# Reordering the start of a fused token-mixing and feed-forward kernel, and signalling its last step by tile

## The reference

```python
W = cond_weights[itok]                          # [32, 64, 64], picked out of [16, 64, 64]
y = einsum('bct,bcd->bdt', x, W)                # mixes the 64 rows of each sample
h = gelu(y @ inter_w + inter_b)                 # [1024] -> [4096], tanh approximation
out = x + h @ output_w + output_b               # [4096] -> [1024]
```

## Time and profile before

| | us |
|---|---|
| median of 3 runs (1271.19 to 1271.51) | 1271.4 |
| the profiled execution's own time | 1270.05 |
| its span in the profile | 1268.2 |
| TensorE busy in the span | 1251.0 |
| VectorE busy | 833.9 |
| ScalarE busy | 567.7 |
| GpSimd busy | 188.5 |

### The profile page before, as it was taken

One profiled execution on the slowest core, in us unless ns is written; L12 is line 12 of the kernel. 1 busy time (PEld: TensorE's weight loads), 2 busy tenths in 40 slices (PEclk: granted clock), 3 DMA queues, 4 the chain that ended last, 5 costly groups with the idle time before them and its releaser, 6 DMA issues.

```text
span 1268.2 us, 15308 instructions
## 1 busy us (share of the span) xinstructions
PE 1251.0 (99%) x5634; PEld 1039.4 (82%) x5634; DVE 833.9 (66%) x1086; ACT 567.7 (45%) x969; POOL 188.5 (15%) x94
## 2 busy tenths in 40 slices
PE   6999999999999999999999999999999999999998
PEld 6888888888888888888888888888888888888886
DVE  5888688676477777757656555555547767774764
ACT  3755445454444444444434444444444444444442
POOL 5242233212000000000033233222200000000000
PEclk9999999999999999999999999999999999999999
DMA  9396566763998232239835335553199942233531
GB/s 348 111 323 227 211 225 249 265 238 144 355 400 322 100 99 90 94 138 391 305 116 191 112 125 183 183 182 131 78 334 395 349 135 90 98 100 100 166 124 43
DMA packets 94941, 249.54 MB, mean 197 GB/s; under 512 B 8307, under 2 KB 16531, under 8 KB 93459
## 3 DMA queue, kind: packets, MB, share of 16 engines
q1 hardware_dynamic: 93778, 248.28, 54.1%
q10 hardware_dynamic: 1088, 0.28, 0.1%
HBM read 162.55 MB, written 85.98 MB: 196 GB/s over the span
## 4 chain that ended last, share of the span: by engine, by line
PE 95%; DVE 3%; DMA 1%; issue 1%; ACT 0%; SPq 0%; DVEq 0%; ACTq 0%
PE ps L558 48%; PE ps L542 45%; DVE lhs L774 1%; PE ps L502 1%; DVE y L763 1%; DMA y_mem<-y_out 1%; PE ps L487 1%; DMA x<-in_x_dram 0%; DVE hs L788 0%; DVE c L781 0%; ACT lhs L620 0%; DVE y_out L876 0%; ACT y_whole L589 0%; DVE acc L849 0%; ACT y L609 0%
## 5 line engine op out<-in xcount | busy, mean ns | idle before, releaser
L542 PE MATMUL ps<-y,lhs 128*128 128x512 f32 x2688 | 611.6, 389 | 2.8 <-ACT y_whole L589 1.5
L558 PE MATMUL ps<-rhs,lhs 128*128 128x512 f32 x2688 | 609.6, 389 | 0.0
L542 PEld LDWEIGHTS ps<-y,lhs 128*128 128x128 f32 x2688 | 503.9, 188 | 108.3 <-ACT y_whole L589 1.6
L558 PEld LDWEIGHTS ps<-rhs,lhs 128*128 128x128 f32 x2688 | 504.5, 188 | 104.8
L690 ACT ACTIVATE lhs<-h_raw 128x512 fp32r<-128x512 f32 x224 | 141.6, 632 | 345.8 <-PE ps L558 340.2
L833 DVE TENSOR_TENSOR lhs<-h_raw,lhs 128x512 fp32r<-128x512 f32 x224 | 155.0, 692 | 188.5 <-ACT lhs L690 188.5
L774 DVE TENSOR_TENSOR lhs<-w_raw,lhs 128x512 fp32r<-128x512 f32 x128 | 117.9, 922 | 127.7 <-ACT lhs L620 127.6
L620 ACT ACTIVATE lhs<-w_raw 128x512 fp32r<-128x512 f32 x128 | 80.8, 632 | 165.6 <-PE ps L542 161.8
L836 DVE TENSOR_TENSOR rhs<-W,rhs 128x512 fp32r<-128x512 f32 x224 | 153.3, 684 | 0.0
L774 DVE TENSOR_TENSOR lhs<-s_w,lhs 128x512 fp32r<-128x512 f32 x96 | 90.2, 940 | 88.2 <-ACT lhs L620 88.1
L458 POOL TENSOR_TENSOR s_w<-w_raw 128x1024 f32<-128x1024 f32 x16 | 48.1, 3008 | 636.7 <-PE ps L558 354.0
(11 more groups left out here) (34 smaller groups left out, 291.6 us busy)
## 6 DMA issues: line engine op xcount, KB each, us to landing
h_raw<-h_mem SPq DMA_DIRECT2D x112, 512.0 KB, 3.4
w_raw<-in_L_ffn_inter_w_dram SPq DMA_DIRECT2D x32, 1024.0 KB, 8.8
h_mem<-hs SPq DMA_DIRECT2D x64, 512.0 KB, 4.7
W<-in_L_ffn_output_w_dram SPq DMA_DIRECT2D x32, 1024.0 KB, 12.6
h_mem<-c SPq DMA_DIRECT2D x48, 512.0 KB, 5.8
y_mem<-y_out SPq DMA_DIRECT2D x28, 512.0 KB, 3.2
y<-y_mem SPq DMA_DIRECT2D x7, 2048.0 KB, 13.0
x<-in_x_dram SPq DMA_DIRECT2D x16, 512.0 KB, 12.3
```

What stands on the lines that cost most here:

```text
L542: last = nc.tensor.matmul(ps[:, bank, :], w[:, k, :], y[i][:, part, k, :], start=(i in FRESH and k == 0 and u == 0), stop=(k == KH - 1 and ...
L558: last = nc.tensor.matmul(ps[:, bank2(h, j, tb), :], lhs[s % RING][:, a, blk(tb)], rhs[r][:, w, :], start=(j in FRESH and q == 0 and u == ...
```

## The change

It has four parts.

1. The half of `cond_all` that SP issued goes to ACT, which now issues both. SP issues all eight tiles `x0` ahead of the first group's weights.
2. POOL waits, ahead of its four sums of the first group, until the first two chunks' weights have been split (`lhs_lo >= 2`).
3. The bias is turned behind the first chunk instead of ahead of all matmuls, with a wait until DVE has copied out all its banks of the mixing (it reuses bank 7). DVE's copy of it moves behind the first `y_sum`; `cond1(1)`, which writes that bank, waits for the copy.
4. In the last step of the kernel, TensorE signals after each of the four token blocks (`tile_done`), and each of DVE's last four additions waits for its own block. That step no longer counts in `step_done`.

```diff
--- before.py
+++ after.py
@@ -137,6 +137,7 @@
         cond_done = sem("cond_done")
         cond1_done = sem("cond1_done")
         step_done = sem("step_done")
+        tile_done = sem("tile_done")
 
         kept_act = sem("kept_act")
         y1_taken = sem("y1_taken")
@@ -305,11 +306,9 @@
                 sp.dma_start(y[i][:].bitcast(F32), y_mem[i]).then_inc(y_in[i], 16)
 
             sp.dma_start(itok_sb[0:1], itok.rearrange("(o b) -> o b", o=1)).then_inc(itok_in, 16)
-            sp.dma_start(cond_all[0:C], cond_w.rearrange("s c d -> c s d")).then_inc(cond_in, 16)
             for j in range(TILES):
                 sp.dma_start(x0[:, j, :], x_tok[0, :, j, :]).then_inc(x0_in[j], 16)
-                if j == TB - 1:
-                    load_w1(0, 0)
+            load_w1(0, 0)
             for j in range(TILES):
                 if j == TILES - 2:
                     sp.wait_ge(cond_done, 2 * KB)
@@ -455,6 +454,7 @@
                         pool.wait_ge(step_done, step2(h - 1, PRODUCTS, -2))
                     else:
                         pool.wait_ge(cond_done, KB)
+                        pool.wait_ge(lhs_lo, 2)
                     nc.gpsimd.tensor_tensor(s1_w[:], a21, a22, ALU.add).then_inc(s_made[0], 1)
                     if g > 0:
                         pool.wait_ge(lhs_lo, step1(h, g - 1, 6))
@@ -493,6 +493,8 @@
 
                 pe.wait_ge(x1_in[j], 16)
                 pe.wait_ge(picked1, PER * (j + 1))
+                if j == 1:
+                    pe.wait_ge(b1_ready, 1)
                 if j < 2:
                     pe.wait_ge(kept_act, KB)
                     pe.wait_ge(kept_dve, KB)
@@ -503,6 +505,13 @@
                                             wdiag[:, TILES + j, :], start=True, stop=True)
                     if kb % KH == KH - 1:
                         last.then_inc(cond1_done, 1)
+
+            def turn_b1():
+                pe.wait_ge(b1_in, 16)
+                pe.wait_ge(ident_made, 1)
+                pe.wait_ge(kept_dve, KB)
+                nc.tensor.matmul(ps[:, 7, 0:F // P], b1_rows[0:F // P], ident[0:F // P],
+                                 start=True, stop=True).then_inc(b1_turned, 1)
 
             def first(h, g, c):
                 i, p = divmod(c, 2)
@@ -558,19 +567,20 @@
                         last = nc.tensor.matmul(ps[:, bank2(h, j, tb), :], lhs[s % RING][:, a, blk(tb)], rhs[r][:, w, :],
                                                 start=(j in FRESH and q == 0 and u == 0),
                                                 stop=(q == PAIRS - 1 and u == 2), skip_group_check=True)
-                last.then_inc(step_done, 1)
-
-            pe.wait_ge(b1_in, 16)
-            pe.wait_ge(ident_made, 1)
-            nc.tensor.matmul(ps[:, 7, 0:F // P], b1_rows[0:F // P], ident[0:F // P], start=True, stop=True).then_inc(b1_turned, 1)
+                    if step2(h, j, q) == PASSES * STEPS - 1:
+                        last.then_inc(tile_done, 1)
+                if step2(h, j, q) < PASSES * STEPS - 1:
+                    last.then_inc(step_done, 1)
+
             pe.wait_ge(wdiag_zero, 2)
-            pe.wait_ge(b1_ready, 1)
             for n in range(2):
                 cond(n)
             for h in range(PASSES):
                 for g in range(NG):
                     for c in range(CHUNKS):
                         first(h, g, c)
+                        if (h, g, c) == (0, 0, 0):
+                            turn_b1()
                         if (h, g) == (0, 0):
                             for j in range(TILES):
                                 if BEHIND[j] == c:
@@ -708,7 +718,8 @@
                     act.wait_ge(y1_kept[item % 2], 16 * (item // 2))
                 nc.scalar.activation(y1_out[item % 2][:, 0, :], y1_in[:, (0, 0, 0, 3, 1, 2, 2)[i], :], ACT.Copy).then_inc(y1_hi, 1)
 
-            act.dma_start(cond_all[C:P], cond_w.rearrange("s c d -> c s d")).then_inc(cond_in, 16)
+            for rows in (slice(0, C), slice(C, P)):
+                act.dma_start(cond_all[rows], cond_w.rearrange("s c d -> c s d")).then_inc(cond_in, 16)
             act.dma_start(b1_rows[0:F // P], b1.rearrange("(a p) -> a p", p=P)).then_inc(b1_in, 16)
             act.wait_ge(ident_made, 1)
             nc.scalar.activation(table_ahead[0:F // P, 0:1], ident[0:F // P, 0:1], ACT.Gelu_apprx_tanh)
@@ -839,7 +850,10 @@
             def add2(h, j, u, tiles):
 
                 m, n = QUARTER[j]
-                dve.wait_ge(step_done, step2(h, j, PAIRS))
+                if step2(h, j, PAIRS) == PASSES * STEPS:
+                    dve.wait_ge(tile_done, (u + 1) * tiles)
+                else:
+                    dve.wait_ge(step_done, step2(h, j, PAIRS))
                 if j < 2 and u == 0:
                     for i in range(TILES):
                         dve.wait_ge(x_in[i], 16 * (h + 1))
@@ -876,8 +890,6 @@
                 nc.vector.tensor_tensor(o[:, 1, :], y1_in[:, (0, 0, 0, 3, 1, 2, 2)[i], :], o[:, 0, :].bitcast(F32),
                                         ALU.subtract).then_inc(y1_split, 1)
 
-            dve.wait_ge(b1_turned, 1)
-            nc.vector.tensor_copy(b1_col[:], ps[:, 7, 0:F // P]).then_inc(b1_ready, 1)
             dve.wait_ge(itok_in, 16)
             dve.wait_ge(cond_in, 32)
             for i in range(2, TILES * PER, 3):
@@ -891,6 +903,8 @@
             dve.wait_ge(kept_act, KB)
             dve.wait_ge(kept_dve, KB)
             y_sum(t1_y, b12, b11)
+            dve.wait_ge(b1_turned, 1)
+            nc.vector.tensor_copy(b1_col[:], ps[:, 7, 0:F // P]).then_inc(b1_ready, 1)
             y_low(1)
             for h in range(PASSES):
                 for g in range(NG):
```

## The result

| | before | changed |
|---|---|---|
| median, six runs each | 1270.93 us | 1276.8 us |
| lowest to highest | 1270.25 to 1271.51 | 1275.63 to 1279.4 |
| profiled execution, its span | 1268.2 | 1276.6 |

The ratio is 1.0047, with a 95% interval of 1.0034 to 1.006. The profiled execution of the changed kernel is the slowest of the six (1279.4). Forecast was 1268.0; the time lies where rival A put it, at a smaller price.

The account below looks back on a forecast made before the run. TensorE's unbroken matmuls were taken as the bound, so only the two ends could change: 1.3 us at the start plus 2.1 at the end, 3.4 us, median 1271.4 to 1268.0; range 1266.0 to 1272.5.

Parts of the forecast that it names:

- rival A: Start, slower: cond_w's small packets starve beside token packets and land at about 18.5 us; time 1279.5 us; chance 0.20.
- the one on cond_w: cond_w wholly on ACT's queue: its second half's landing taken as unchanged; it may slip 1.7 us before DVE's copies decide.
- `cond(1)` follows `cond(0)` with no gap: Token mixing at the start: with tokens ahead of the weights, PE's 1.61 us stall before `cond(1)` goes.
- `y_low(0)` and `low1` run free: DVE at the start: undisturbed by GpSimd's sums, `y_low(0)` takes 2.40 us, ending at about 21.0, and `low1` ends at 22.3.
- The contention moves: Before the third chunk: GpSimd's sums delay `y_sum` and `y_low(1)` instead; three sums of four still meet DVE.
- The stall before the third chunk: PE ahead of the third chunk: it waits 2.6 us for DVE, the stalls before chunks 1 and 2 being gone.
- The bias: Its matmul pair of 0.63 us, moved behind the first chunk, lies in PE's slack: costs nothing, at most 0.6 us.
- no stall stands at the picks: 12 picks behind GpSimd's last sum, from about 34.5 us: no cost; they cost something from a delay of about 5 us.
- The end: Behind the last matmul: three of four additions and their stores run under PE; gain 2.1 us, at least 1.86.
- the 1.3 us at the third chunk: Start of the kernel: the third chunk begins at 36.80 instead of 38.11 us; gain 1.3 us, range 0.75 to 1.7.
- the start of the first sum: GpSimd's first sum near the kernel's start: taken as 22.4 us, between bounds of 22.0 and 22.96.
- Rival B: Start pays nothing: sums one GpSimd turn longer (2.22 us), or PE returns from idling at the lower clock (1.3 us); chance 0.22.

Follow-up runs that it names:

- experiment 1: The changed kernel with cond_w's first half back on SP, ahead of the token tiles: 1269.36 us, ratio 0.9987.
- the wait alone: The kernel before with the signal by tile at the end and, of the start, only the added wait ahead of the sums: 1270.3 us, ratio 1.0.

## Why the prediction was wrong

**The step that failed** is the one on cond_w: "What is open is when the second half of cond_w lands; the sum takes it as unchanged." It landed at 14.05 instead of 5.9. The mechanism stood beside it as rival A with 0.20, since no row told packets from bytes; nothing in the rows spoke against it, so it deserved more, and the bound "it may slip 1.7 us" should have been set against a stream of 10 us of tokens. Of rival A's own terms the count was off. It had 98 small packets per engine left when the tokens began, alternating to 18.5. In fact 1068 passed between 4 and 6 us, 804 of them in one microsecond in which the tokens nearly paused, which no rival had; one for one is seen only from about 6. So TensorE started 4.4 us earlier than A's 19.9, and the time is 2.7 under its 1279.5.
**Steps that held.** `cond(1)` follows `cond(0)` with no gap (both are one row of 128 records). `y_low(0)` and `low1` run free. The contention moves to `y_sum` and `y_low(1)`. The stall before the third chunk is 2.89 (2.6 was forecast). The bias costs the third chunk nothing that shows (29.37 against 29.24 us behind the first matmul), and no stall stands at the picks. The end gives 2.0 us (2.1 was forecast).

**Terms off in size.** Of the 1.3 us at the third chunk, 0.28 came, in experiment 1. From the start of the first sum to that chunk the working had 14.4 us, and it took 14.5 (23.33 to 37.83). What was 0.9 off is the start of the first sum, taken as 22.4. `low1` ended at 22.80, since VectorE's first copies began 8.23 us behind the first matmul (7.48 in the profile of before). And GpSimd started 0.53 behind it, a delay that the prediction had left out.

**Rival B was real too**, beside A. It had the stall bring TensorE back at the lower clock, at 1.3 us and 0.22. "TensorE: Matmul & The Clock Gate" of the Trainium skill (the HAM clock gate) says as much of idle stretches, and the windows agree: 0.50 behind 2.89 us. It cost 2.7 us in the profile of the changed kernel and nothing in that of experiment 1, with the same stall. It was taken for one case of several; it comes on top of whichever case holds. With cond_w left on SP, the forecast of 1268.0 would have met 1269.4; five of its ten runs show a mean clock of 1.0, four of these at 1267.5 to 1267.9.

## What to carry to other kernels

Before small-packet transfers go to a second queue, ask what streams in the first: here 0.5 MB in 256-byte packets waited 8 us beside 4 KB packets, and all work hung on it. Where TensorE is the bound, price a stall of 2 to 4 us at more than its length and look at the spread of the runs: filling it with discarded matmuls paid here, and so did removing it. When a wait is moved, read each engine's list for what stands behind it; it took two edits to turn the later sums into time.

## What was not expected of the hardware

- Half-row transfers on the busy queue, with packets of 2 instead of 4 KB, brought the small packets home 5.9 us earlier (8.16 instead of 14.05), more than half of their delay. A large part of them passed while the busy queue nearly paused (804 from 5 to 6 us in the changed kernel), not in turns with it.
- Behind the same stall of 2.89 us the granted clock was 0.50 in one profile and stayed at 1.00 in another (experiment 1, from 38 to 45 us). The ten runs of experiment 1 lie from 1267.46 to 1272.16, with mean clocks from 1.0 to 0.997.
- The clock can fall after TensorE is back at work: in the kernel with the wait alone, from about 38.4 us, when it had run since 36.97.
- A GpSimd sum starts 0.5 us behind the VectorE instruction that ends its wait (22.80 to 23.33 in experiment 1, 21.99 to 22.51 with the wait alone).
